# Output transposes of an attention kernel replaced by ones between V's columns and a swap of rows by DMA

## The chip, the cores and the metric

The kernel runs on one core of a Trainium2 chip. The core has five engines, each with its own queue of instructions that it works off in order: TensorE (PE in the profile, with its weight loads as PEld), VectorE (DVE), ScalarE (ACT), GpSimd (POOL) and SyncE (SP), which here only issues DMAs. They wait for each other through semaphores. The metric is the device time of one execution in microseconds; lower is better.

## What is computed

Cross-attention over 8 batches, 112 query rows, 375 key rows, width 256, 16 heads of 16 channels, all in 32-bit floats:

```python
Q = (x @ Wq.T + bq)      # per batch [112, 256], 16 heads of 16
K = (ctx @ Wk.T + bk)    # per batch [375, 256]
V = (ctx @ Wv.T + bv)    # per batch [375, 256]
scores = einsum('bhqd,bhkd->bhqk', Q, K) / sqrt(16)
attn = softmax(scores, axis=-1)
context = einsum('bhqk,bhkd->bhqd', attn, V)   # heads side by side: [112, 256]
z = context @ W_o.T + b_o + x
out = (z - mean(z)) / sqrt(var(z) + 1e-5) * gamma + beta   # over the 256 columns
```

## The kernel before

The work goes batch by batch (index `i`, 0 to 7), and a batch is cut into 12 units (`u`): 4 groups of 4 heads, each over 3 chunks of 125 key rows. In each unit TensorE computes one tile of scores with the keys on the partitions (L975, into `st_bank`), from which ScalarE makes the exponentials (L633, into `p_tile`, the tile that the profile calls `pw`). Beside that TensorE computes, some 17 heads ahead, the scores with the queries on the partitions (L942, into three `mx_bank`s), of which VectorE takes the maximum of each row (L748). The maxima of a batch are transposed (L957, "MT"), split in two parts and sent by DMA into a row of `q_stack` (L358), so that the scores of L975 come out already shifted by the maximum.

The projections of later batches lie between these: V of batch `i + 2` in units 2 to 4, K of batch `i + 3` in units 8 and 10 (L881). ScalarE takes each half of a K and rounds it (L545, L549), GpSimd subtracts (L430), and SyncE stacks the parts by DMA (L326) at the start of the next batch.

The product with V (L993) has 4 heads side by side in the array: head `j` of a group uses the array's columns from `32*j` on, with 16 columns of V and one column of ones (VW = 17), so that partition `32*j + 16` of `pv_bank` is the softmax denominator. In the batches 0 to 5 the products of two groups stand together in units 7 and, for the batch before, 1 (48 instructions); in batches 6 and 7 one group at a time (24 instructions).

What comes behind, for the batch whose products ended in unit 1 of the next batch: ScalarE copies `pv_bank` to `o_raw` (L604); TensorE transposes its four groups (L1004, "OT", in unit 6); VectorE takes the reciprocal of the 16 denominators of a row and multiplies (L770, L772, `normalise`); TensorE transposes the two halves back (L1012, mostly in front of MT, otherwise "ONT"); ScalarE copies them with V's bias to `o_normT` (L623); TensorE projects (L1025, "OUT", three batches later in unit 0; in the end sooner); VectorE adds the residual and takes mean and variance (L781 to L785); GpSimd does the rest of the layer norm (L450 to L467) and SyncE stores (L336).

The last batch but one ends inside batch 7: its last product with V is in unit 2, OUT(6) in unit 11. Batch 7's own output goes another way (L1037 to L1057), in quarters and halves. The order on every engine is written out by hand: loops over `i` and `u`, with tables that say which step stands in which unit (`U_OUT`, `U_OT`, `U_MT`). Two PSUM banks are handed from job to job in the order of `M0_JOBS` and `M1_JOBS`; a job waits until the one before it in its bank was read.

## Time and profile before

| | |
|---|---|
| median of 3 runs (141.05 to 143.31) | 141.18 us |
| the profiled execution | 142.0 us |
| its span, first to last instruction | 140.1 us |
| PE busy | 129.5 us (92%), 1477 instructions |
| DVE busy | 96.6 us (69%) |
| ACT busy | 90.1 us (64%) |
| POOL busy | 81.9 us (58%) |
| chain that ended last | PE 73%, SPq 9%, DVE 7%, DMA 5% |
| granted TensorE clock, mean | 0.993 |

Engines are named as above; SPq is SyncE's issuing of DMAs. A row of the timeline has its start and its length in microseconds from the span's start; instructions of one kind that follow each other are one row, with their count. On TensorE the lengths overlap, since a matmul's end is modelled, so the distance from one start to the next tells what a step costs. A 32-bit matmul is two instructions there (so L993 has 24 for the 12 matmuls of a group).

### The profile page before, as it was taken

Reading aid. Unit: us, or ns where it says so; the run is one execution under the profiler, and the core shown is the slowest. Engines: PE = TensorE matmul, PEld = TensorE weight load, DVE = VectorE, ACT = ScalarE, POOL = GpSimd, SP = SyncE. Lnnn points to the kernel's source line nnn. Section 1 sums busy time; section 2 is a strip of 40 time slices with the busy share of each in tenths; the row PEclk is TensorE's granted clock in tenths of the full one; section 3 lists DMA queues with packets and bytes.
Section 4 is the critical chain, followed back from the end, with each engine's and each line's share of the span. In section 5 each row is a group of like instructions: output and inputs, shape, how many; then the busy total and the mean of one; then the engine's idle time right before and its main releaser. Section 6 shows DMA issues by size and latency. Waiting matters only on the chain.

```text
span 140.1 us, 3936 instructions
## 1 busy us (share of the span) xinstructions
PE 129.5 (92%) x1477; PEld 113.6 (81%) x1477; DVE 96.6 (69%) x225; ACT 90.1 (64%) x187; POOL 81.9 (58%) x105
## 2 busy tenths in 40 slices
PE   4999997699999999998999999999999999999960
PEld 4799965589788979797989998999899888878720
...
GB/s 146 317 347 255 231 296 129 297 238 187 54 185 285 272 126 70 218 135 98 68 120 215 5 72 188 256 120 72 90 276 0 25 19 5 8 36 33 37 0 66
DMA packets 16099, 19.59 MB, mean 140 GB/s; under 512 B 2624, under 2 KB 15488, under 8 KB 16080
## 3 DMA queue, kind: packets, MB, share of 16 engines
...
q10 hardware_dynamic: 480, 0.28, 0.7%
q8 instruction: 12, 0.20, 0.7%
...
## 4 chain that ended last, share of the span: by engine, by line
PE 73%; SPq 9%; DVE 7%; DMA 5%; issue 3%; ACTq 1%; ACT 1%; POOLq 0%; DVEq 0%
PE m_bank L881 16%; PE pv_bank L993 14%; PE st_bank L975 14%; PE mx_bank L942 13%; PE m_bank L1025 4%; SPq L326 4%; SPq L266 4%; DMA q_stack<-shift_half 3%; PE m_bank L1004 2%; PE mx_bank L975 2%; DMA q_stack<-shift 2%; DVE k_stack L725 2%; DVE mx L748 2%; PE m_bank L902 1%; PE m_bank L1012 1%
## 5 line engine op out<-in xcount | busy, mean ns | idle before, releaser
L748 DVE TENSOR_REDUCE mx<-mx_bank 112x1 f32<-112x375 f32 x128 | 63.7, 541 | 22.3 <-PE mx_bank L942 21.9
L633 ACT ACTIVATE pw<-st_bank 125x448 f32<-125x448 f32 x86 | 45.1, 546 | 18.1 <-PE st_bank L975 17.8
L942 PE MATMUL mx_bank<-k_stack,q_stack 128*112 128x376 f32 x128 | 43.3, 352 | 0.2
L975 PE MATMUL st_bank<-q_stack,k_stack 128*125 128x224 f32 x172 | 34.9, 284 | 2.3 <-DMA q_stack<-shift_half 1.8
L975 PEld LDWEIGHTS st_bank<-q_stack,k_stack 128*125 128x125 f32 x172 | 28.5, 186 | 6.1 <-issue 3.6
L942 PEld LDWEIGHTS mx_bank<-k_stack,q_stack 128*112 128x112 f32 x128 | 22.0, 176 | 3.4 <-DVE mx L748 1.7
L430 POOL TENSOR_TENSOR k_hl<-k_full,k_hl 128x376 fp32r<-128x376 f32 x10 | 10.0, 1001 | 20.2 <-ACT k_hl L549 20.2
L993 PE MATMUL pv_bank<-pw,v_sb 125*17 125x112 f32 x744 | 21.5, 260 | 0.0
L993 PEld LDWEIGHTS pv_bank<-pw,v_sb 125*17 125x17 f32 x744 | 16.7, 97 | 3.1 <-issue 1.9
L881 PE MATMUL m_bank<-w_hl,c_hl 128*125 128x256 f32 x126 | 18.2, 282 | 0.0
L404 POOL TENSOR_TENSOR c_hl<-c_raw,c_hl 128x752 fp32r<-128x752 f32 x6 | 11.1, 1854 | 10.5 <-ACT c_hl L520 10.5
L881 PEld LDWEIGHTS m_bank<-w_hl,c_hl 128*125 128x125 f32 x126 | 17.3, 186 | 0.0
L881 PE MATMUL m_bank<-c_hl,w_hl 128*128 128x376 f32 x84 | 16.6, 335 | 0.3 <-DVE shift L755 0.3
L881 PEld LDWEIGHTS m_bank<-c_hl,w_hl 128*128 128x128 f32 x84 | 14.5, 188 | 0.5 <-DVE shift L755 0.5
L450 POOL TENSOR_SCALAR var_eps<-mv 112x1 f32<-112x1 f32 x7 | 1.6, 232 | 13.1 <-DVE mv L785 13.1
L461 POOL TENSOR_SCALAR yo<-z,mv,rstd 112x256 f32<-112x256 f32 x7 | 8.7, 1236 | 0.8
L559 ACT COPY v_sb<-m_bank 125x512 f32<-125x512 f32 (+1 forms) x14 | 6.8, 482 | 2.4 <-PE m_bank L881 1.9
L545 ACT ACTIVATE k_full<-m_bank,bqk 128x376 f32<-128x376 f32 x10 | 5.8, 576 | 3.8 <-PE m_bank L881 3.8
L1025 PE MATMUL m_bank<-wo,o_normT 128*112 128x256 f32 x28 | 7.4, 385 | 0.0
L604 ACT COPY o_raw<-pv_bank 128x448 f32<-128x448 f32 x7 | 3.7, 534 | 5.3 <-PE pv_bank L993 5.3
L781 DVE TENSOR_TENSOR z<-m_bank,x_space 112x256 f32<-112x256 f32 x7 | 2.9, 415 | 5.8 <-PE m_bank L1025 5.8
L633 ACT ACTIVATE pw<-mx_bank 125x448 f32<-125x448 f32 x10 | 5.3, 567 | 1.4 <-PE mx_bank L975 1.4
...
## 6 DMA issues: line engine op xcount, KB each, us to landing
...
```

What stands on the lines that cost most here:

```text
L404: nc.gpsimd.tensor_tensor(c_hl[b % 2][:, 1, :, :], c_raw[b % 2][:, :, :], c_hl[b % 2][:, 0, :, :].bitcast(F32), op=ALU.subtract).then_inc( ...
L430: nc.gpsimd.tensor_tensor(k_hl[b % 2][:, 1, t, :], k_full[:, t, :], k_hl[b % 2][:, 0, t, :].bitcast(F32), op=ALU.subtract).then_inc(k_lo, 1)
L461: nc.gpsimd.tensor_scalar(yo[b % 2][:, :], z[b % 2][:, :], mv[b % 2][:, 0:1], rstd[:, 0:1], op0=ALU.subtract, op1=ALU.mult).then_inc(y_rea ...
L545: nc.scalar.activation(k_full[:, t, :], src[:, 0:KVP], ACT.Identity, bias=bqk[:, 2 + t:3 + t]).then_inc(k_taken, 1)
L559: nc.scalar.copy(v_sb[b % VR][0:KC, c0:c0 + chunks, :, 0:DK], src[0:KC, 0:chunks * D].rearrange("p (c h d) -> p c h d", c=chunks, h=H)).th ...
L633: nc.scalar.activation(p_tile[0:KC, n % PR, :, :], st_of(n)[0:KC, 0:4 * Q].rearrange("p (j q) -> p j q", j=4), ACT.Exp, scale=float(DK) ** ...
L748: nc.vector.tensor_reduce(mx[b % 2][:, h % 2, q_pair(h // 2):q_pair(h // 2) + 1], mx_bank[n % MR][0:Q, 0:KV], axis=AX_X, op=ALU.max, negat ...
L881: last = nc.tensor.matmul(dst, lhs(a, e), rhs(c, e), start=(k + e == 0), stop=(k == len(PRODUCTS) - 1 and e == EC - 1))
L942: nc.tensor.matmul(mx_bank[n % MR][0:Q, 0:KVP], q_stack[k][:, side, q_pair(h // 2), b - Q_STACKS[k][0], :], k_stack[b % 3][:, h // 2, :], ...
L975: last = nc.tensor.matmul(st_of(n)[0:KC, k * 2 * Q:(k + 1) * 2 * Q], k_stack[i % 3][:, 2 * g + k, c * KC:(c + 1) * KC], q_stack[qk][:, :, ...
L993: last = nc.tensor.matmul(pv_of(b, g)[32 * j:32 * j + VW, g * Q:(g + 1) * Q], v_sb[b % VR][0:KC, c, 4 * g + j, :], p_tile[0:KC, (UNITS * b ...
L1025: last = nc.tensor.matmul(dst[0:Q, D:2 * D], o_normT[b % 2][:, k, :], wo[:, k, :], start=(k == 0), stop=(k == EC - 1))
```

## The change

V's tile gets 32 columns a head instead of 17: each of the 16 columns of V is followed by a column of ones (`VW = 2 * DK`). In `pv_bank` each even partition then holds a channel and the odd one behind it the denominator of the same head. The transposes OT and ONT and `normalise` go for batches 0 to 6. In their place, for batch `b`:

- ScalarE copies the whole bank to `o_raw` (`take_raw`, unit 1 of the next batch), then groups 0 and 2 to `o_normT` and groups 1 and 3 to `den` (`take_o`, unit 2). For batch 6 VectorE does all three (`take_o_last`, unit 2 of batch 7).
- SyncE sends two DMAs (`swap_rows`): the odd rows of groups 0 and 2 (denominators) into the even rows of `den`, and the even rows of groups 1 and 3 (channels) into the odd rows of `o_normT`. Then `o_normT` has 128 channels on its partitions, in an order for which the rows of W_o and the bias of V are permuted on the host, and `den` their denominators.
- VectorE takes the reciprocal of `den`, 128x224 (`invert`, unit 8; for batch 6 in unit 4 of batch 7).
- GpSimd multiplies and adds V's bias (`scale_output`), between its two subtractions for K.
- TensorE projects in unit 1, two batches later, in front of the products with V (for batch 4 in unit 8 of batch 6, for batch 5 in unit 5 of batch 7, for batch 6 in unit 11 of batch 7 as before). MT moves to unit 7, in front of the products with V (unit 4 in batch 6).

Ones are written once: VectorE's memset of the first V tile in two pieces, ScalarE's copy of the ones to the second, GpSimd's memset of the third. The memsets of `pv_bank` and `mx_bank` go, since all 128 partitions are now written. In batch 7, `normalise_last` has one reciprocal and one product for each group.

```diff
-VW = DK + 1
+VW = 2 * DK
...
-U_OUT, U_OT, U_Q, U_CONTEXT = 0, 6, 11, 5
+U_OUT, U_LN, U_Q, U_CONTEXT, U_NORM = 1, 1, 11, 5, 8
 U_K = ((9, 11), (8, 10))
 U_V = (2, 3, 4)
 HALF = UNITS // 2
-NORM_WITH = {3: 0, 4: 1, 5: 2, 6: 3, 7: 5}
-U_MT = (8, 7, 6, 6, 6, 6, 5)
+U_MT = (8, 7, 7, 7, 7, 7, 4)
+OUT_AT = {i: U_OUT for i in range(2, B - 2)} | {B - 2: 8, B - 1: 5}
+NORM_AT = {i: U_LN for i in range(2, B - 2)} | {B - 2: 8, B - 1: 5}
...
-    if _i >= 3:
-        M1_JOBS.append(("OUT", _i - 3))
+    if _i >= 2:
+        M0_JOBS.append(("OUT", _i - 2))
     M0_JOBS.append(("V", _i + V_AHEAD, 0))
     M1_JOBS.append(("V", _i + V_AHEAD, 1))
-    M0_JOBS.append(("MT", _i + 1))
-    M1_JOBS.append(("OT", _i - 1))
+    M1_JOBS.append(("MT", _i + 1))
...
-        v_sb = [sb(f"v_sb{i}", [PART, NC, H, VW]) for i in range(VR)]
+        v_sb = [sb(f"v_sb{i}", [PART, NC, H, DK, 2]) for i in range(VR)]
...
+            def swap_rows(b):
+
+                sp.wait_ge(o_raw_ready, b + 1)
+                raw = o_raw[b % 2][:, :].rearrange("p (e s q) -> p e s q", e=EC, s=2)
+                sp.dma_start(den[0:PART - 1:2, :, :], raw[1:PART:2, :, 0, :]).then_inc(swap_in[b % 2], 16)
+                sp.dma_start(o_normT[b % 2][1:PART:2, :, :], raw[0:PART - 1:2, :, 1, :]).then_inc(swap_in[b % 2], 16)
+
             for i in range(B):
                 if 1 <= i < B - V_AHEAD:
                     for t in range(2):
                         stack_k(i + V_AHEAD, t)
+                if i >= 1:
+                    swap_rows(i - 1)
...
+            nc.gpsimd.memset(v_sb[2][:, :, :, :, :], 1.0).then_inc(v_ones[2], 1)
...
+            def scale_output(b):
+
+                pool.wait_ge(rden_ready, b + 1)
+                nc.gpsimd.tensor_tensor(o_normT[b % 2][:, :, :], o_normT[b % 2][:, :, :], den[:, :, :],
+                                        op=ALU.mult).then_inc(o_scaled, 1)
+                pool.wait_ge(o_scaled, b + 1)
+                pool.wait_ge(bv_in, 16)
+                for e in range(EC):
+                    last = nc.gpsimd.tensor_scalar(o_normT[b % 2][:, e, :], o_normT[b % 2][:, e, :], bv[:, e:e + 1], None,
+                                                   op0=ALU.add)
+                last.then_inc(o_normT_ready, 1)
...
+                if 2 <= i < 2 + B // ROWS:
+                    bias_into_x(i - 2)
                 if i + AHEAD + 1 < B:
                     context_lo(i + AHEAD + 1)
                 if i == 0:
                     stack_q(pool, 2, 1)
                 if i + AHEAD < B:
-                    for t in range(2):
-                        subtract_k(i + AHEAD, t)
-                if 2 <= i < 2 + B // ROWS:
-                    bias_into_x(i - 2)
+                    subtract_k(i + AHEAD, 0)
+                if i >= 1:
+                    scale_output(i - 1)
+                if i + AHEAD < B:
+                    subtract_k(i + AHEAD, 1)
                 if i == 2:
                     clear_q()
             for b in range(B - V_AHEAD - 3, B - 1):
                 inverse_deviation(b)
                 scale_rows(b)
+                if b + 2 < B - 1:
+                    scale_output(b + 2)
...
-            def take_o(b):
+            def take_raw(b):
 
                 act.wait_ge(pv_done, NG * (b + 1))
                 if b >= 2:
-                    m, n = m_job("OT", b - 2)
-                    act.wait_ge(m_full[m], n + 1)
-                nc.scalar.copy(o_raw[b % 2][:, :], pv_bank[:, 0:NG * Q]).then_inc(o_raw_ready, 1)
+                    act.wait_ge(swap_in[b % 2], 32 * (b // 2))
+                nc.scalar.copy(o_raw[b % 2][:, :], pv_bank[:, 0:NG * Q])
+
+            def take_o(b):
+
+                src = pv_bank[:, 0:NG * Q].rearrange("p (e s q) -> p e s q", e=EC, s=2)
+                if b >= 2:
+                    wait_full(act, "OUT", b - 2)
+                nc.scalar.copy(o_normT[b % 2][:, :, :], src[:, :, 0, :])
+                if b >= 1:
+                    act.wait_ge(o_scaled, b)
+                nc.scalar.copy(den[:, :, :], src[:, :, 1, :]).then_inc(o_raw_ready, 1)
 
             def take_first_half():
...
-                    if u == (1 if i < B - 1 else 2) and i >= 1:
+                    if u == 1 and 1 <= i < B - 1:
+                        take_raw(i - 1)
+                    if u == 2 and 1 <= i < B - 1:
                         take_o(i - 1)
...
-            def normalise(b):
-
-                src = wait_full(dve, "OT", b)[0:Q, :].rearrange("p (h c) -> p h c", h=H)
-                nc.vector.reciprocal(rden[:, :, :], src[:, :, DK:VW]).then_inc(rden_ready, 1)
-                dve.wait_ge(rden_ready, b + 1)
-                nc.vector.tensor_tensor(o_norm[b % 2][:, :, :], src[:, :, 0:DK],
-                                        rden[:, :, :].to_broadcast([Q, H, DK]), op=ALU.mult
-                                        ).then_inc(o_norm_ready, 1)
+            def take_o_last():
+
+                b = B - 2
+                dve.wait_ge(pv_done, NG * (b + 1))
+                dve.wait_ge(swap_in[b % 2], 32 * (b // 2))
+                nc.vector.tensor_copy(o_raw[b % 2][:, :], pv_bank[:, 0:NG * Q])
+                src = pv_bank[:, 0:NG * Q].rearrange("p (e s q) -> p e s q", e=EC, s=2)
+                wait_full(dve, "OUT", b - 2)
+                nc.vector.tensor_copy(o_normT[b % 2][:, :, :], src[:, :, 0, :])
+                dve.wait_ge(o_scaled, b)
+                nc.vector.tensor_copy(den[:, :, :], src[:, :, 1, :]).then_inc(o_raw_ready, 1)
+
+            def invert(b):
+                dve.wait_ge(swap_in[b % 2], 32 * (b // 2 + 1))
+                nc.vector.reciprocal(den[:, :, :], den[:, :, :]).then_inc(rden_ready, 1)
...
+                    if u == U_NORM and 1 <= i < B - 1:
+                        invert(i - 1)
+                    if i == B - 1 and u == 2:
+                        take_o_last()
+                    if i == B - 1 and u == 4:
+                        invert(B - 2)
+                    if i >= 2 and u == NORM_AT[i]:
+                        layer_norm(i - 2)
+                    if i == B - 1 and u == 8:
                         layer_norm(B - 2)
...
-                                                v_sb[b % VR][0:KC, c, 4 * g + j, :],
+                                                v_sb[b % VR][0:KC, c, 4 * g + j, :, :].rearrange("k d s -> k (d s)"),
...
+                    if i + 1 < B and u == U_MT[i]:
+                        transpose_max(i + 1)
+                    if i >= 2 and u == OUT_AT[i]:
+                        out_project(i - 2)
...
-                    if u == U_OUT and i >= 3:
-                        out_project(i - 3 if i < B - 1 else B - 3)
-                    if u == 2 and i == 6:
-                        transpose_o_norm(4)
-                    if u == 3 and i == 6:
-                        transpose_o(5)
-                    if u == 5 and i == 6:
-                        out_project(4)
-                    if i + 1 < B and u == U_MT[i]:
-                        transpose_max(i + 1)
-                    if u == U_OT and 1 <= i <= 5:
-                        transpose_o(i - 1)
-                    if u == 4 and i == B - 1:
-                        transpose_o(B - 2)
-                    if u == 6 and i == B - 1:
-                        transpose_o_norm(B - 2)
...
-        "woT": w_o.T,
+        "woT": by_output(w_o.T),
```

TensorE's row in batch 4, units 6 and 7 (st_bank: scores; mx_bank: scores for the maximum; o_norm and o_raw: ONT and OT; mx: MT; pv_bank: products with V). Before:

```order
L942 MATMUL mx_bank<-k_stack,q_stack 112x376
L1012 MATMUL m_bank<-ident,o_norm 128x112 x2
L957 MATMUL m_bank<-ident,mx 16x112
L1004 MATMUL m_bank<-ident,o_raw 112x128 x4
L975 MATMUL st_bank<-q_stack,k_stack 125x224 x2
L942 MATMUL mx_bank<-k_stack,q_stack 112x376
L993 MATMUL pv_bank<-pw,v_sb 17x112 x24
```

and now:

```order
L999 MATMUL st_bank<-q_stack,k_stack 125x224 x2
L968 MATMUL mx_bank<-k_stack,q_stack 112x376
L981 MATMUL m_bank<-ident,mx 16x112
L1017 MATMUL pv_bank<-pw,v_sb 32x112 x24
L999 MATMUL st_bank<-q_stack,k_stack 125x224 x2
```

The six transposes are gone, MT stands in front of the products, and these have 32 rows out.

GpSimd's row from the end of batch 4 to batch 5 (k_hl: the two subtractions for K of batch 7; x_space: the output bias into the residual). Before:

```order
L430 TENSOR_TENSOR k_hl<-k_full,k_hl 128x376 x2
L437 TENSOR_TENSOR x_space<-x_space,bo_rows 112x256 x2
L450 TENSOR_SCALAR var_eps<-mv 112x1
```

and now:

```order
L445 TENSOR_TENSOR x_space<-x_space,bo_rows 112x256 x2
L438 TENSOR_TENSOR k_hl<-k_full,k_hl 128x376
L481 TENSOR_TENSOR o_normT<-o_normT,den 128x224
L486 TENSOR_SCALAR o_normT<-o_normT,bv 128x112 x2
L438 TENSOR_TENSOR k_hl<-k_full,k_hl 128x376
L458 TENSOR_SCALAR var_eps<-mv 112x1
```

The scaling of batch 3's output stands behind the first of K's subtractions, and TensorE's OUT(3) in unit 1 of batch 5 waits for it.

TensorE's row at the end, batch 7 from unit 8 on (o_normT: OUT(6)). Before:

```order
L975 MATMUL st_bank<-q_stack,k_stack 125x224 x2
L993 MATMUL pv_bank<-pw,v_sb 17x112 x12
L975 MATMUL st_bank<-q_stack,k_stack 125x224 x2
L975 MATMUL mx_bank<-q_stack,k_stack 125x224 x4
L1025 MATMUL m_bank<-wo,o_normT 112x256 x2
L993 MATMUL mx_bank<-pw,v_sb 17x112 x12
L1037 MATMUL m_bank<-ident,o_raw 112x128 x2
```

and now:

```order
L999 MATMUL st_bank<-q_stack,k_stack 125x224 x2
L1017 MATMUL pv_bank<-pw,v_sb 32x112 x12
L999 MATMUL st_bank<-q_stack,k_stack 125x224 x2
L999 MATMUL mx_bank<-q_stack,k_stack 125x224 x4
L1029 MATMUL m_bank<-wo,o_normT 112x256 x2
L1017 MATMUL mx_bank<-pw,v_sb 32x112 x12
L1041 MATMUL m_bank<-ident,o_raw 112x128 x2
```

OUT(6) keeps its place; what makes its input is now VectorE's three copies, two DMAs, a reciprocal and three GpSimd operations.

## Rows read from the trace of the kernel before

**Rows 1.** Windows: busy us (instructions) of each engine, then granted clock, DMA share.
```profile
100.00:125.00 25.00, 25.00 (x362) 21.54 (x364) 17.79 (x44) 17.62 (x40) 13.75 (x20) 1.00 0.18 59
125.00:140.00 15.00, 10.27 (x152) 7.00 (x140) 5.07 (x19) 6.76 (x17) 7.99 (x12) 0.94 0.11 32
```

**Rows 2.** Timeline of TensorE, batch 2, unit 6: start, length, then what.
```profile
63.93 0.38 PE L1012 MATMUL m_bank<-ident,o_norm 112*128 112x112 f32 x2 [0.37 <-issue]
64.15 0.26 PE L957 MATMUL m_bank<-ident,mx 112*16 112x112 f32 x1
```

**Rows 3.** Chain of work that ended last, batch 2: start, length, what.
```profile
64.41 0.44 PE m_bank L1004 x4
```

**Rows 4.** Groups by line and shape, weight loads: busy us, mean ns, idle before.
```profile
L993 PEld LDWEIGHTS pv_bank<-pw,v_sb 125*17 125x17 f32 x744 | 16.7, 97 | 3.1 <-issue 1.9 <-ACT pw L633 0.6
...
L975 PEld LDWEIGHTS st_bank<-q_stack,k_stack 128*125 128x125 f32 x172 | 28.5, 186 | 6.1 <-issue 3.6 <-ACT pw L633 1.1 <-DMA q_stack<-shift 0.8
```

**Rows 5.** Groups by line and shape, the other engines.
```profile
L437 POOL TENSOR_TENSOR x_space<-x_space,bo_rows 112x256 f32<-112x256 f32 x8 | 5.7, 734 | 0.0
...
L772 DVE TENSOR_TENSOR o_norm<-m_bank,rden 112x256 f32<-112x256 f32 x7 | 3.0, 424 | 0.2
...
L770 DVE RECIPROCAL rden<-m_bank 112x16 f32<-112x16 f32 x7 | 1.7, 243 | 1.4 <-PE m_bank L1004 1.4
...
L208 ACT COPY o_raw<-pv_bank 128x224 f32<-128x224 f32 x1 | 0.4, 381 | 0.0
...
L208 DVE COPY o_raw<-mx_bank 128x112 f32<-128x112 f32 x1 | 0.3, 254 | 0.0
...
L833 DVE RECIPROCAL rden<-m_bank 112x4 f32<-112x4 f32 x1 | 0.2, 183 | 0.1
```

**Rows 6.** Timelines: GpSimd's first subtraction and TensorE's products in unit 1.
```profile
54.57 1.02 POOL L430 TENSOR_TENSOR k_hl<-k_full,k_hl 128x376 fp32r<-128x376 f32 x1 [3.26 <-ACT k_hl L549]
57.45 1.34 PE L993 MATMUL pv_bank<-pw,v_sb 125*17 125x112 f32 x48
...
69.35 1.00 POOL L430 TENSOR_TENSOR k_hl<-k_full,k_hl 128x376 fp32r<-128x376 f32 x1 [3.19 <-ACT k_hl L549]
72.89 1.34 PE L993 MATMUL pv_bank<-pw,v_sb 125*17 125x112 f32 x48
...
98.65 1.00 POOL L430 TENSOR_TENSOR k_hl<-k_full,k_hl 128x376 fp32r<-128x376 f32 x1 [5.61 <-ACT k_hl L549]
101.67 1.34 PE L993 MATMUL pv_bank<-pw,v_sb 125*17 125x112 f32 x48
```

**Rows 7.** Timelines of ScalarE and TensorE, batch 6, units 1 to 4.
```profile
115.78 0.53 ACT L604 COPY o_raw<-pv_bank 128x448 f32<-128x448 f32 x1 [0.93 <-PE pv_bank L993]
116.32 0.55 ACT L633 ACTIVATE pw<-st_bank 125x448 f32<-125x448 f32 x1
...
117.60 0.77 PE L993 MATMUL pv_bank<-pw,v_sb 125*17 125x112 f32 x24
```

**Rows 8.** Timelines of all engines, batches 6 and 7, to the end.
```profile
120.26 1.14 SPq L358 DMA_DIRECT2D q_stack<-shift  x2
...
121.63 0.23 POOL L450 TENSOR_SCALAR var_eps<-mv 112x1 f32<-112x1 f32 x1 [1.58 <-DVE mv L785]
...
124.55 0.77 PE L993 MATMUL pv_bank<-pw,v_sb 125*17 125x112 f32 x24
...
125.46 0.23 POOL L450 TENSOR_SCALAR var_eps<-mv 112x1 f32<-112x1 f32 x1
...
130.03 1.03 PE L1025 MATMUL m_bank<-wo,o_normT 128*112 128x256 f32 x4
130.99 0.77 PE L993 MATMUL mx_bank<-pw,v_sb 125*17 125x112 f32 x24
...
137.26 0.48 DVE L860 SCALAR_TENSOR_TENSOR yo<-yo,rstd,be_rows 112x256 f32<-112x256 f32 x1 [0.40 <-POOL rstd L453]
```

**Rows 9.** DMAs by line: KB each, median us from issue to landing.
```profile
q_stack<-q_first SPq DMA_DIRECT2D x3, 56.0 KB, 2.3
```

More of the change, by code:

```diff
@@ L83 @@
         M0_JOBS.append(("Q", 3, _i - 1))
-M0_JOBS += [("OT", 5), ("MT", 7), ("OT", 6), ("OT_LAST", 0), ("OT_LAST", 2)]
-M1_JOBS += [("OUT", 3), ("ONT", 4), ("OUT", 4), ("OUT", 5), ("ONT", 6), ("OUT", 6), ("OUT", B - 1)]
+M0_JOBS += [("OUT", 4), ("OT_LAST", 0), ("OT_LAST", 2)]
+M1_JOBS += [("MT", 7), ("OUT", 5), ("OUT", 6), ("OUT", B - 1)]
 S0_JOBS += [("ONT_HALF", 0), ("ONT_HALF", 1)]
@@ L140, in build @@
         rden = sb("rden", [Q, H, 1])
-        o_norm = [sb(f"o_norm{i}", [Q, H, DK]) for i in range(2)]
+        o_norm = sb("o_norm", [Q, EC, 4, DK, 2])
+        den = sb("den", [PART, EC, Q])
         o_normT = [sb(f"o_normT{i}", [PART, EC, Q]) for i in range(2)]
@@ L174, in build @@
         ident_clear, ident_ready = sem("ident_clear"), sem("ident_ready")
-        pv_clear = sem("pv_clear")
         k_ones = [sem(f"k_ones{i}") for i in range(3)]
         q_clear = [sem(f"q_clear{k}") for k in range(NQ)]
-        v_ones = sem("v_ones")
+        warm_ready, v_ones = sem("warm_ready"), [sem(f"v_ones{i}") for i in range(VR)]
         m_full = [sem(f"m_full{i}") for i in range(len(JOBS))]
@@ L186, in build @@
         o_raw_ready, rden_ready = sem("o_raw_ready"), sem("rden_ready")
-        o_norm_ready, o_normT_ready = sem("o_norm_ready"), sem("o_normT_ready")
+        o_scaled, o_normT_ready = sem("o_scaled"), sem("o_normT_ready")
+        swap_in = [sem(f"swap_in{i}") for i in range(2)]
         xb_ready = sem("xb_ready")
@@ L615, in take_half_t @@
                                      bias=bv[:, k:k + 1]).then_inc(half_normT, 1)
-            def take_o_norm_t(b, *job):
-                src = wait_full(act, *job)
-                if job[0] == "MT":
-                    act.wait_ge(shift_ready, job[1] + 2)
-                act.wait_ge(bv_in, 16)
-                for k in range(EC):
-                    last = nc.scalar.activation(o_normT[b % 2][:, k, :], src[:, k * Q:(k + 1) * Q], ACT.Identity,
-                                                bias=bv[:, k:k + 1])
-                last.then_inc(o_normT_ready, 1)
             for i in range(B):
@@ L738, in _ @@
             context_lo(1)
-            for i in range(1, VR):
-                nc.vector.memset(v_sb[i][:, :, :, DK:VW], 1.0).then_inc(v_ones, 1)
             for t in range(2):
@@ L830, in normalise_last @@
                 g0, n = LAST[k].start, LAST[k].stop - LAST[k].start
[L831 to L833 removed]
+                src = (wait_full(dve, "OT_LAST", k)[0:Q, 0:n * PART]
+                       .rearrange("p (g j d s) -> p g j d s", g=n, j=4, s=2))
+                scale = rden[:, 4 * g0:4 * (g0 + n), :].rearrange("p (g j) x -> p g j x", g=n)
+                to = o_norm[:, g0 // 2, :, :, g0 % 2:g0 % 2 + n].rearrange("p j d s -> p s j d")
+                for g in range(n):
+                    last = nc.vector.reciprocal(scale[:, g], src[:, g, :, 0, 1:2])
+                last.then_inc(rden_ready, 1)
                 dve.wait_ge(rden_ready, B + k)
[L835 to L837 removed]
+                for g in range(n):
+                    last = nc.vector.tensor_tensor(to[:, g], src[:, g, :, :, 0], scale[:, g].to_broadcast([Q, 4, DK]),
+                                                   op=ALU.mult)
+                last.then_inc(last_norm, 1)
             dve.wait_ge(pv_done, NG * (B - 1) + LAST[1].stop)
[L840 removed]
+            dve.wait_ge(swap_in[(B - 1) % 2], 32 * ((B - 1) // 2))
             take_last(nc.vector.tensor_copy, 1)
@@ L998, in values @@
                     last.then_inc(pv_done, 1)
-            def transpose_o(b):
-                dst, full = claim("OT", b)
-                pe.wait_ge(o_raw_ready, b + 1)
-                for g in range(NG):
-                    last = nc.tensor.transpose(dst[0:Q, g * PART:(g + 1) * PART],
-                                               o_raw[b % 2][:, g * Q:(g + 1) * Q], ident[:, :])
-                last.then_inc(full, 1)
-            def norm_columns(dst, b):
-                pe.wait_ge(o_norm_ready, b + 1)
-                flat = o_norm[b % 2][:, :, :].rearrange("q h d -> q (h d)")
-                for k in range(EC):
-                    last = nc.tensor.transpose(dst[:, k * Q:(k + 1) * Q], flat[:, k * PART:(k + 1) * PART],
-                                               ident[0:Q, 0:Q])
-                return last
-            def transpose_o_norm(b):
-                dst, full = claim("ONT", b)
-                norm_columns(dst, b).then_inc(full, 1)
             def out_project(b):
@@ L1144, in by_stack, with by_output @@
     return a.reshape(2, 4, 2, DK, *rest).transpose(0, 2, 3, 1, *range(4, 4 + len(rest))).reshape(D, *rest)
+def by_output(a):
+    rest = a.shape[1:]
+    return a.reshape(EC, 2, 4, DK, *rest).transpose(0, 2, 3, 1, *range(4, 4 + len(rest))).reshape(D, *rest)
 def kernel(x, ctx_1024, L0_xattn_W_qkv, L0_xattn_b_qkv, L0_xattn_W_o, L0_xattn_b_o, L0_xattn_ln_gamma,
```

59 lines of the change are left out of this document (13 added, 46 removed).

## The prediction, written before the changed kernel was run

> **What bounds the kernel now.** I read the page first, then the chain of waits, then TensorE's timeline batch by batch, then each queue that the change touches. In the windows TensorE is busy through all of 100 to 125 us at the granted clock 1.00, its level of 2.4 GHz, while VectorE, ScalarE and GpSimd stand at 18, 18 and 14 of 25 us [rows 1]. The page's slices show the same from the second quarter of the span on. So an instruction taken from TensorE in this stretch is worth its whole length, and a wait put into TensorE's row costs its whole length. After 125 us TensorE is busy 10.3 of 15 us [rows 1]: there the end is a chain through several engines, and lengths of steps count, whoever does them.
>
> **What goes from TensorE.** ONT's two transposes are 0.22 us from start to start [rows 2], OT's four are 0.44 us on the chain [rows 3]: 0.66 us a batch. In front of ONT in batch 2 TensorE also stood 0.37 us for the head maxima [rows 2]; MT one unit later no longer meets that. Up to batch 6 OT of batches 0 to 4 and ONT of 0 to 3 go: 5 x 0.44 + 4 x 0.22 + 0.37 = 3.45 us.
>
> **Wider weights.** The stationary tile of a product with V has 32 columns instead of 17. A load of 17 columns takes 97 ns, one of 125 takes 186 [rows 4]: 0.82 ns a column, so 12 ns more for each of 768 loads (744 in this row, 24 in another bank). But 24 loads of 97 ns are 2.3 us, and the 24 products with their loads take 0.77 us [rows 8], so loads run under matmuls of the other three heads. At the least this costs nothing; if each load showed its 12 ns it would be 9.4 us. I take the first load of each of some 20 bursts, 0.25 us, since the row with the same array layout hides its loads. The Trainium skill says (TensorE: Matmul & The Clock Gate, LDWEIGHTS (loading the stationary operand)) that a load takes columns / 1.2 ns: 14 ns for 17, 27 for 32, an estimate; all 768 exposed would then come to 9.6 us. The trace's rows have nearly the same slope on a far larger constant, and do not show the loads exposed [rows 4, 8].
>
> **A new wait in unit 1.** OUT(i-2) needs `scale_output(i-2)`, which GpSimd does after the first subtraction for K, and this waits for K's projection in unit 8. `scale_output`: one product over 224 columns, 0.70 us (256 columns take 0.734 [rows 5]); two additions over 112 columns, for which no row is near; with one input and half the columns they lie between 0.37 and 0.73, and I take 0.48; 0.2 us for three handoffs. Sum 1.86 us, bounds 1.6 to 2.4. In batch 5 TensorE would start OUT(3) where the products now start, less the OUT that leaves unit 0 (0.96 us from start to start [rows 8]): 101.67 - 0.96 = 100.7. GpSimd is ready at 98.65 + 1.00 + 1.86 = 101.5 [rows 6]. TensorE waits 0.8 us, and the products, which stand behind OUT, with it. Batch 4 has the same spacing. In batches 2 and 3 a projection of Q lengthens the unit before: 54.57 + 1.02 + 1.86 = 57.45, just when the products start now (batch 2 has no OUT in unit 0 to lose), so nothing; 69.35 + 1.00 + 1.86 = 72.2 against 72.89 - 0.96 = 71.9, 0.3 us [rows 6]. Together 1.9 us. Each GpSimd price off by 0.3 us moves this by up to 1 us. VectorE's reciprocal in unit 8 ends before GpSimd asks for it.
>
> **Batch 6.** The products of its first group need the bank empty. ScalarE's first copy starts at 115.78 and takes 0.53, an exponential 0.55 [rows 7], then two copies of 0.38 each (128x224 took 0.381 [rows 5]): 117.6 us, when the products start now [rows 7]. So the 0.66 us of transposes in front of them gain nothing. Behind them go ONT(5), 0.22, and OUT(5), which moves past the last products of batch 6: 1.18 us. In batches 1 to 5 ScalarE's 0.76 us more lie in its idle time before unit 3.
>
> **At the end of batch 6's products (E).** They end at 124.55 + 0.77 = 125.3 us now [rows 8]; then at 125.3 - 3.45 - 1.18 + 0.25 + 1.9 = 122.8.
>
> **From E to OUT(6).** VectorE's copies: 112 columns take 0.254, 256 take 0.424 [rows 5], so 0.65 for 448 and 0.39 for each 224: 1.43 us. SyncE issues two DMAs, 0.57 each [rows 8], and the second lands 2.3 us after its issue began, as the DMA of rows of the same length does [rows 9]: 2.87. The reciprocal: 4 columns 183 ns, 16 columns 243 [rows 5], 5 ns a column, so 1.28 us for 224; at the least it runs like a copy, 0.39. `scale_output` 1.86, handoffs 0.2. Sum 7.64 us: OUT(6) starts at 130.5, against 130.03 now [rows 8]. TensorE's own work between is 4.7 - 0.66 + 0.96 = 5.0 us, so it stands idle for 2.6 us, and the last products with V are behind OUT(6) in its row. OUT(6) is 0.45 us later than now.
>
> **GpSimd's backlog.** `scale_output(6)` stands in front of two layer norms of 125.46 - 121.63 = 3.83 us each [rows 8], which start only then: 7.7 us, and then comes the last deviation, 0.6 us, for which VectorE's last operation waits. It starts 8.2 us after OUT(6) starts, against 137.26 - 130.03 = 7.23 now [rows 8]: 1.0 us.
>
> **Edits without cost.** The memsets and the copy of ones run before the data has arrived or beside it. GpSimd's third memset delays K(2) on TensorE, which at that place waits for the first shift anyway; without that cover it would cost its own length. SyncE's two issues stand behind K's stacking and, in batch 6, ahead of the shift for batch 7, 1.14 us for such a pair [rows 8]; the shift then still has seven units until it is asked for. `bias_into_x` moves into GpSimd's idle time.
>
> **Sum.** 0.45 + 1.0 = 1.45 us later. The profiled execution of 142.0 us (span 140.1) would become 143.4; it stands 0.8 over the median of the runs, 141.18, so the forecast is 142.6 us, 1% slower: what is taken from TensorE comes back as waits for GpSimd and at the end.
>
> **Rivals.**
> 1. *The waits are short.* Reciprocal like a copy (-0.9), additions at 0.37 (-0.2 from E to OUT(6), -0.2 in each of three batches): -1.7, 140.9 us, and 139.8 if the additions cost still less. For: the rows of the reciprocal read single PSUM elements far apart, and the slope may be that of the reading. Against: GpSimd's chain in batches 4 and 5 is late with any price of the additions. Chance 0.20.
> 2. *All of it is saved*: no wait in unit 1, and the way from E to OUT(6) is covered. 7 x 0.66 + 0.37 = 5.0 us: 136.2. This needs the 7.64 us to fit into 5.0, by two missing terms at once. Chance 0.04.
> 3. *The wider weights show.* If the four loads of a round cannot overlap, each round grows by one load's 12 ns or all four: 2.4 to 9.4 us, 145 to 152 us. It decides from the point where four loads no longer fit under one round of matmuls. Chance 0.08.
> 4. *The clock falls in the wait before OUT(6).* TensorE stands still for 2.6 us there, and in the last stretch the granted clock is already 0.94 on average [rows 1]; at 1.2 GHz OUT(6) alone takes 0.96 us more, and with the products and transposes behind it some 3 us: 146. Against: TensorE's present waits leave the clock full up to 125 us [rows 1]. The Trainium skill (TensorE: Matmul & The Clock Gate, Part 1: The HAM clock gate) has the clock halved after a stretch without matmuls. This trace shows a fall only in its last stretch [rows 1]. Chance 0.08.
>
> **How the numbers follow.** The forecast's case has the remaining 0.60, with 141.0 to 144.6 as its own range (the reciprocal and the additions up or down by half of their bounds). This kernel's measurement can tell about 2%, 138.4 to 144.0 us, from no change. Faster: rival 2 and a little, 0.05. Slower: rivals 3 and 4 and the upper fifth of the forecast's case, 0.28. The rest, 0.67, is no change. The range goes from the lower end of rival 1 to the lower ends of 3 and 4: 139.8 to 145.6.
>
> **What would show it.** Right: TensorE's OUT rows in batches 4 and 5 preceded by 0.5 to 1.2 us of idle time that GpSimd's `o_normT` ends; idle time of 2 to 3 us before OUT(6); VectorE's reciprocal of `den` near 1.3 us; GpSimd's last power 8 us behind OUT(6). Wrong: rounds of the products with V above their present pace (0.77 us for 24), reciprocals of 0.4 us, OUT in unit 1 without idle time, or a granted clock below 1.00 before 125 us.

## The result: 5.3% slower

The changed kernel takes 149.54 us (median of 4 runs, 147.66 to 149.67), the kernel before 141.28 us on the same chip: ratio 1.0531, 95% interval 1.0466 to 1.0596. The ratio is an estimate of its own and not the quotient of the two medians (1.058). Ratios leave out runs in a slower state, more than 1.5% above the fastest of their kernel. The profiled execution took 149.67 us, its span is 147.9 us (140.1 before). The windows of [rows 1], of the changed kernel (TensorE, weight loads, VectorE, ScalarE, GpSimd, clock):

```profile
100.00:125.00 25.00, 22.84 (x321) 18.48 (x319) 17.34 (x35) 16.54 (x37) 13.41 (x20) 1.00 0.21 70
125.00:148.00 23.00, 14.36 (x172) 9.63 (x164) 9.02 (x28) 7.30 (x17) 14.45 (x22) 0.85 0.09 26
```

TensorE, busy all of the first window before, stands 2.2 of 25 us; the second has grown from 15 to 23 us, and its clock is 0.85 on average. What TensorE waited for from 41 to 131 us, in waits of over 0.15 us (total us, times, longest):

```profile
PE st_bank L999 <- ACT pw L659: 1.3, 2, 0.7
PE mx_bank L968 <- DVE mx L767: 1.0, 1, 1.0
PE st_bank L999 <- DMA q_stack<-shift: 0.4, 1, 0.4
PE m_bank L1029 <- DVE q_hl L733: 0.3, 2, 0.2
PE m_bank L981 <- DVE mx L767: 0.3, 1, 0.3
```

None of these is GpSimd's `o_normT`. The first two are the places to look at. Unit 1 of batch 5, TensorE, ScalarE and GpSimd (start, length, what, idle time before it):

```profile
100.87 0.51 PE L968 MATMUL mx_bank<-k_stack,q_stack 128*112 128x376 f32 x2
102.02 0.48 PE L999 MATMUL st_bank<-q_stack,k_stack 128*125 128x224 f32 x2 [0.65 <-ACT pw L659]
102.34 0.34 PE L968 MATMUL mx_bank<-k_stack,q_stack 128*112 128x376 f32 x1
102.58 1.09 PE L1029 MATMUL m_bank<-wo,o_normT 128*112 128x256 f32 x4
103.60 1.36 PE L1017 MATMUL pv_bank<-pw,v_sb 125*32 125x112 f32 x48
...
100.42 0.57 ACT L570 ACTIVATE k_full<-m_bank,bqk 128x376 f32<-128x376 f32 x1
101.02 0.51 ACT L574 CAST k_hl<-k_full 128x376 fp32r<-128x376 f32 x1
101.43 1.65 ACT L659 ACTIVATE pw<-st_bank 125x448 f32<-125x448 f32 x3
...
101.36 1.12 POOL L486 TENSOR_SCALAR o_normT<-o_normT,bv 128x112 f32<-128x112 f32 x2
```

The same place in the kernel before:

```profile
100.06 1.12 PE L1025 MATMUL m_bank<-wo,o_normT 128*112 128x256 f32 x4
100.83 0.53 PE L942 MATMUL mx_bank<-k_stack,q_stack 128*112 128x376 f32 x1
101.19 0.37 PE L975 MATMUL st_bank<-q_stack,k_stack 128*125 128x224 f32 x2
101.41 0.34 PE L942 MATMUL mx_bank<-k_stack,q_stack 128*112 128x376 f32 x1
```

ScalarE works off two conversions of K (1.1 us) before the exponentials of units 11 and 0 free the next `st_bank`. Before, OUT lay between the scores of units 0 and 1 and covered just this time; now it stands behind them, and TensorE waits 0.65 us bare. GpSimd's `o_normT` was ready at 102.48, only 0.1 us too late, because the other wait had come first. Without that wait TensorE would have come to OUT some 0.65 us sooner, at about 101.9 (an estimate from these rows), and would have stood nearly as long for GpSimd: two waits lie beside each other here.

A shorter wait of the same kind, below the list's 0.15 us, stands in unit 7 of the batches 2 to 5. In batch 5, first before, with MT and six transposes ahead of the unit's scores, then in the changed kernel:

```profile
107.62 0.36 PE L1012 MATMUL m_bank<-ident,o_norm 112*128 112x112 f32 x2
...
108.26 0.46 PE L975 MATMUL st_bank<-q_stack,k_stack 128*125 128x224 f32 x2
```

```profile
109.37 0.34 PE L968 MATMUL mx_bank<-k_stack,q_stack 128*112 128x376 f32 x1
109.78 0.48 PE L999 MATMUL st_bank<-q_stack,k_stack 128*125 128x224 f32 x2
110.10 0.33 PE L968 MATMUL mx_bank<-k_stack,q_stack 128*112 128x376 f32 x1
```

From 109.37 to 109.78 are 0.41 us where the pace is 0.17, and the unit's two score instructions take 0.32 where two take 0.21: 0.34 us lost, though TensorE stood only 0.07 us for an exponential (the trace names ScalarE). Before, the transposes lay over this time.

And the end of batch 5 on VectorE:

```profile
112.43 0.55 DVE L767 TENSOR_REDUCE mx<-mx_bank 112x1 f32<-112x375 f32 x1 [0.95 <-PE mx_bank L968]
112.89 1.54 DVE L800 RECIPROCAL den<-den 128x224 f32<-128x224 f32 x1
114.35 1.84 DVE L767 TENSOR_REDUCE mx<-mx_bank 112x1 f32<-112x375 f32 x4
```

The reciprocal stands in front of four head maxima; no projections are left in this batch with which TensorE could pass the time, all three `mx_bank`s fill, and it stands 1.0 us. VectorE had idled 0.95 us just before.

The changed operations by line and shape (busy us, mean ns), to be read beside [rows 4, 5]:

```profile
L1017 PEld LDWEIGHTS pv_bank<-pw,v_sb 125*32 125x32 f32 x744 | 17.6, 111 | 4.6 <-issue 2.6 <-ACT pw L659 1.4
L800 DVE RECIPROCAL den<-den 128x224 f32<-128x224 f32 x7 | 10.8, 1547 | 6.5 <-DMA o_normT<-o_raw 6.5
L486 POOL TENSOR_SCALAR o_normT<-o_normT,bv 128x112 f32<-128x112 f32 x14 | 7.8, 568 | 0.7
L481 POOL TENSOR_TENSOR o_normT<-o_normT,den 128x224 f32<-128x224 f32 x7 | 4.7, 666 | 13.4 <-DVE den L800 13.4
```

The chain of waits from batch 6's last products to OUT(6):

```profile
125.97 0.76 PE pv_bank L1017 x24
...
126.75 0.62 DVE o_raw L791
127.38 0.30 DVE o_normT L794
127.68 0.31 DVE den L796
...
128.00 0.67 SPq L363
...
128.71 3.04 DMA o_normT<-o_raw
...
135.38 2.02 PE m_bank L1029 x4
```

Between 131.8 and 135.4 come the reciprocal (1.55 us) and GpSimd's three operations (1.87). TensorE ran out of work at 131.5. The clock (the number ahead of the DMA share) in that wait, and from OUT(6) on:

```profile
131.50:133.50 2.00, 0.01 (x1) 0.00 (x0) 1.72 (x2) 1.27 (x4) 0.08 (x1) 1.00 0.19 57
135.50:140.50 5.00, 5.00 (x55) 3.09 (x55) 1.92 (x8) 0.00 (x0) 4.46 (x7) 0.50 0.07 23
```

The clock fell from 1.00 to 0.50 (2.4 to 1.2 GHz) at about 134.7 us, while TensorE stood still, and came back at about 141.1, when it had been at work since 135.4. OUT(6) takes 2.02 us where it took 1.03 [rows 8].

**Where the 7.8 us of span came from.** Batch 6's products end at 126.7 (125.3 before): +1.4. From there to OUT(6) 8.65 us instead of 4.7: +3.95. From OUT(6) to the end 12.5 instead of 10.1: +2.4. The first part by kinds of TensorE's work, from batch 1 to the end of batch 6's products. Each instruction counts from the end of the one before it to its own end, both as the profile models them, and idle time stands apart; predicted for idle time are 1.9 in unit 1 and 0.66 in batch 6, less the 0.37 of [rows 2]:

| us | before | after | predicted change | change |
|---|---|---|---|---|
| transposes OT, ONT | 4.15 | 0 | -3.96 | -4.15 |
| OUT (6 before, 5 after) | 5.37 | 5.11 | -0.96 | -0.26 |
| MT | 0.67 | 0.90 | 0 | +0.23 |
| products with V | 16.85 | 17.01 | +0.25 | +0.16 |
| scores | 35.86 | 38.59 | 0 | +2.73 |
| projections | 20.50 | 20.24 | 0 | -0.26 |
| idle | 0.98 | 3.88 | +2.19 | +2.90 |

The scores' 2.73 us belong for the most part to the waits: the first score behind idle time ends 0.37 us after its start, where one that follows another ends 0.11 us behind it (0.43 and 0.17 for the scores of the maxima), so a wait costs 0.26 us more than its idle time. Twelve scores stand behind idle time in the changed kernel, three before. Nine of the twelve waited for ScalarE's exponentials: 1.7 us idle and nine times 0.26, some 4.1 us together, as much as the transposes gave. The kernel before had one or two such waits, with no more than 0.01 us idle in each.

Distances from one start to the next mislead behind OUT: in front of scores its four instructions take 0.77 us to the next start in the rows above (0.67 in other batches), but the score behind them takes 0.36 to the next start instead of 0.17. From end to end OUT costs 0.86 to 0.96 us in the kernel before, whatever follows it.

### The profile page after: what moved, and what is told of

Its sections match the earlier page's. It is cut to its first block, busy times and chain, and to the rows that moved or that the text cites. A ratio compares the mean times of both kernels' runs of the same rounds, so it can differ in the third digit from the quotient of the medians.

```text
span 147.9 us, 3872 instructions
## 1 busy us (share of the span) xinstructions
PE 130.5 (88%) x1435; PEld 110.8 (75%) x1435; DVE 103.6 (70%) x220; ACT 90.0 (61%) x185; POOL 95.1 (64%) x127
## 4 chain that ended last, share of the span: by engine, by line
PE 54%; DVE 12%; ACT 9%; issue 9%; POOL 8%; DMA 4%; ACTq 1%; SPq 1%; POOLq 0%; DVEq 0%
PE pv_bank L1017 13%; PE m_bank L907 13%; PE mx_bank L968 9%; PE st_bank L999 9%; ACT pw L659 5%; PE m_bank L1029 5%; ACT k_full L570 3%; DVE mx L767 3%; POOL q_stack L264 2%; POOL q_stack L406 2%; DMA o_normT<-o_raw 2%; DMA q_stack<-shift 2%; DVE k_stack L746 2%; POOL c_hl L412 1%; DVE den L800 1%
## 5 line engine op out<-in xcount | busy, mean ns | idle before, releaser
L968 PE MATMUL mx_bank<-k_stack,q_stack 128*112 128x376 f32 x128 | 42.0, 348 | 2.7 <-issue 1.5
L1017 PE MATMUL pv_bank<-pw,v_sb 125*32 125x112 f32 x744 | 22.3, 266 | 0.0
L1017 PEld LDWEIGHTS pv_bank<-pw,v_sb 125*32 125x32 f32 x744 | 17.6, 111 | 4.6 <-issue 2.6
L800 DVE RECIPROCAL den<-den 128x224 f32<-128x224 f32 x7 | 10.8, 1547 | 6.5 <-DMA o_normT<-o_raw 6.5
L481 POOL TENSOR_TENSOR o_normT<-o_normT,den 128x224 f32<-128x224 f32 x7 | 4.7, 666 | 13.4 <-DVE den L800 13.4
L1029 PE MATMUL m_bank<-wo,o_normT 128*112 128x256 f32 x28 | 8.5, 430 | 4.2 <-issue 3.9
L630 ACT COPY o_raw<-pv_bank 128x448 f32<-128x448 f32 x6 | 3.2, 534 | 10.0 <-PE pv_bank L1017 10.0
L1029 PEld LDWEIGHTS m_bank<-wo,o_normT 128*112 128x112 f32 x28 | 4.8, 193 | 5.9 <-issue 4.2
L486 POOL TENSOR_SCALAR o_normT<-o_normT,bv 128x112 f32<-128x112 f32 x14 | 7.8, 568 | 0.7
```

The lines of the kernel that those rows point to most:

```text
L486: last = nc.gpsimd.tensor_scalar(o_normT[b % 2][:, e, :], o_normT[b % 2][:, e, :], bv[:, e:e + 1], None, op0=ALU.add)
L800: nc.vector.reciprocal(den[:, :, :], den[:, :, :]).then_inc(rden_ready, 1)
L968: nc.tensor.matmul(mx_bank[n % MR][0:Q, 0:KVP], q_stack[k][:, side, q_pair(h // 2), b - Q_STACKS[k][0], :], k_stack[b % 3][:, h // 2, :], ...
L1017: last = nc.tensor.matmul(pv_of(b, g)[32 * j:32 * j + VW, g * Q:(g + 1) * Q], v_sb[b % VR][0:KC, c, 4 * g + j, :, :].rearrange("k d s -> k ...
L1029: last = nc.tensor.matmul(dst[0:Q, D:2 * D], o_normT[b % 2][:, k, :], wo[:, k, :], start=(k == 0), stop=(k == EC - 1))
```

## Experiments

Ratios are to the kernel before on the same chip, with 95% intervals.

**1. scale_first**: is it GpSimd that is waited for?

```diff
-                if i + AHEAD < B:
-                    subtract_k(i + AHEAD, 0)
                 if i >= 1:
                     scale_output(i - 1)
                 if i + AHEAD < B:
+                    subtract_k(i + AHEAD, 0)
                     subtract_k(i + AHEAD, 1)
```

> GpSimd scales the batch's output before both subtractions of K's low parts instead of between them, so o_normT is ready about 1.0 us (one 999 ns subtraction) earlier. Theory of the prediction: the output projection in unit 1 waits for the scaling, so the changed kernel should gain up to 1.9 us, 149.5 to about 147.6. Theory from its trace (the 0.65 us of TensorE in unit 1 of batches 4 and 5 end with ScalarE's exponentials, not with GpSimd): no change, 149.5 within 0.5 us, and the 0.65 us stay.

Measured 149.04 us, ratio 1.0511 (1.0476 to 1.0546): no gain that can be told from none. The waits of ScalarE's making are unchanged:

```profile
PE st_bank L998 <- ACT pw L658: 1.3, 2, 0.7
```

Units 1 of batches 4 and 5 are 0.14 us shorter, which is all that stood behind GpSimd alone there. Whether TensorE would wait for GpSimd if it did not wait for ScalarE, this run can't tell; experiments 2 and 3 bear on it.

**2. out_before**: the edit of experiment 1, and the projection back behind unit 0's scores.

```diff
-U_OUT, U_LN, U_Q, U_CONTEXT, U_NORM = 1, 1, 11, 5, 8
+U_OUT, U_LN, U_Q, U_CONTEXT, U_NORM = 0, 1, 11, 5, 8
```

> The same earlier scaling, and in batches 2 to 5 the output projection behind unit 0's first scores, where the kernel before had it in batches 3 to 5, not in unit 1. Theory 'lost cover': the projection's 0.96 us on TensorE lay over ScalarE's two K conversions (0.57 + 0.51 us) that stand ahead of the exponentials of unit 0; put back, the 0.65 us of batches 4 and 5 go, and the 0.17 us of batches 2 and 3: 1.6 us less, about 147.9, and unit 1 to unit 2 takes 2.0 us again (3.1 now). Theory 'wait for GpSimd': with the scaling 1.0 us earlier and the projection 1.0 to 1.5 us earlier the wait is as long as before, 149.5, and shows in front of the projection. Third: batch 5's end is set by VectorE (its reciprocal), which gives back part: 148.5.

Measured 149.03 us, 1.0504 (1.0444 to 1.0564): missed. The waits for ScalarE in unit 1 are gone and batches 4 and 5 are 0.3 and 0.5 us shorter, but two others took their place:

```profile
PE m_bank L1028 <- DVE q_hl L732: 2.0, 2, 1.0
...
PE m_bank L1028 <- issue: 0.6, 2, 0.3
```

In batches 2 and 3 OUT's PSUM bank held a projection of Q until VectorE had read it (batches 0.55 us longer each); in 4 and 5 OUT now waits 0.3 us for its input.

**3. out_cover**: the edit of experiment 1, and the projection back in batches 4 and 5 alone.

```diff
-OUT_AT = {i: U_OUT for i in range(2, B - 2)} | {B - 2: 8, B - 1: 5}
+OUT_AT = {2: U_OUT, 3: U_OUT, 4: 0, 5: 0} | {B - 2: 8, B - 1: 5}
```

> The changed kernel with the scaling ahead of both subtractions on GpSimd, and with the output projection behind unit 0's first scores in batches 4 and 5 only (2 and 3 keep unit 1, since there it waited 1.0 us for VectorE's low parts of Q when it was moved). Theory 'cover and GpSimd together': batches 4 and 5 take 0.5 us less each, 149.5 to 148.5, with 0.3 us of wait for GpSimd left in each. If neither wait matters to the end: 149.5.

Measured 148.37 us, 1.0467 (1.0381 to 1.0554): 1.2 us under the changed kernel's median, about as expected, but the intervals overlap. Batches 4 and 5 take 14.88 and 14.02 us from start to start, 15.05 and 14.56 in the changed kernel: the expected 0.5 us came in batch 5 only. OUT still waits 0.3 us for its input in each, with GpSimd's scaling a whole subtraction earlier.

**4. before_out_late**: the same move, alone, in the kernel before.

```diff
-                    if u == U_OUT and i >= 3:
+                    if u == U_OUT and i >= B - 2:
...
+                    if u == U_OUT + 1 and 3 <= i < B - 2:
+                        out_project(i - 3)
                     if i == B - 1 and u in (5, 8, 11):
```

> The kernel before, with one thing changed: in batches 3 to 5 the output projection stands in unit 1 in front of the products with V instead of behind unit 0's scores. No swap, no reciprocal of 224 columns, transposes as before, and the projection's input is ready long ahead. Theory 'lost cover': TensorE stands 0.65 us in unit 1 of batches 4 and 5 for ScalarE's exponentials (as in the changed kernel), and the products with V start 0.25 us later behind the projection than behind scores: 2 x 0.65 + 3 x 0.25 = 2.0 us more, 141.9 to about 143.9. Theory 'only its input was late': no change, 141.9.

Measured 143.82 us, 1.0144 (1.0077 to 1.0210): 2.0 us slower by the ratio, as 'lost cover' had it. Its batch 5 on TensorE, with no swap and no GpSimd in the way:

```profile
101.76 0.48 PE L975 MATMUL st_bank<-q_stack,k_stack 128*125 128x224 f32 x2 [0.66 <-ACT pw L633]
...
102.25 1.02 PE L1025 MATMUL m_bank<-wo,o_normT 128*112 128x256 f32 x4
103.20 1.34 PE L993 MATMUL pv_bank<-pw,v_sb 125*17 125x112 f32 x48
```

The 0.66 us are there. From start to start the batches 3, 4 and 5 are 0.30, 0.82 and 0.80 us longer than before, 1.9 together. The reason is not the expectation's 0.25 us for the place in front of the products: OUT ends 0.86 us behind the score ahead of it in all three, no later than before. It is the waits for ScalarE (0.04, 0.64 and 0.66 us idle) and the 0.26 us that each costs on top.

**5. no_reciprocal**

```diff
-                nc.vector.reciprocal(den[:, :, :], den[:, :, :]).then_inc(rden_ready, 1)
+                nc.vector.reciprocal(den[:, :, 0:1], den[:, :, 0:1]).then_inc(rden_ready, 1)
```

> The reciprocal of the denominators covers 1 column (of 128x224, 1547 ns, seven times), so the outputs of batches 0 to 6 are multiplied by denominators that were mostly not inverted; everything else stands. Theory 'the reciprocal is on the path twice': the 1.0 us that TensorE waits for a head maximum at the end of batch 5 goes, and the wait ahead of the last batch's output projection (3.9 us) shrinks by 1.4 us: 2.4 us less, 147.1, with the clock still falling; if the shorter wait also keeps the granted clock at 1.00, up to 2.4 us more, 144.7. Theory 'hidden, the swap alone counts': under 0.5 us less, 149.0 to 149.5.

Measured 145.98 us, 1.0284 (1.0241 to 1.0326): 3.6 us less, between the two cases of its first theory. The wait for a head maximum is gone; the wait ahead of OUT(6) is 2.6 us, and the clock still falls, but comes back sooner:

```profile
133.00:136.00 3.00, 3.00 (x30) 1.68 (x28) 1.31 (x4) 0.00 (x0) 2.72 (x4) 0.52 0.00 0
136.00:140.00 4.00, 3.39 (x36) 1.79 (x34) 1.78 (x9) 0.96 (x3) 3.54 (x6) 1.00 0.09 29
```

**6. invert_early**

```diff
-U_OUT, U_LN, U_Q, U_CONTEXT, U_NORM = 1, 1, 11, 5, 8
+U_OUT, U_LN, U_Q, U_CONTEXT, U_NORM = 1, 1, 11, 5, 7
```

> VectorE's reciprocal moves from unit 8 to behind the shift in unit 7, where VectorE idles for 0.95 us in batch 5 while TensorE does products with V. Theory 'the reciprocal stands in front of a head maximum at the end of batch 5': of TensorE's 1.0 us there 0.6 to 1.0 us goes, 149.5 to about 148.7. Rival: in batches 2 to 4 it now delays the maximum that ends the next wait and the gain is paid back there, 149.5.

Measured 147.80 us, 1.0345 (1.0245 to 1.0445): 1.7 us less by the medians. The single runs spread too far to weigh that: 146.6, 146.7, 148.9 and 149.3, against 147.7, 149.5, 149.6 and 149.7 of the changed kernel, 1.1 us less at the lowest and 0.4 at the highest. Batch 5 takes 13.53 us instead of 14.56, 1.0 us less, as expected. The rest of the 3.1 us that its profile's span gains lies elsewhere, in what the edit does not touch: batch 1 began 0.6 us sooner, batch 6's second swap DMA landed 2.72 us after its issue (3.04 in the changed kernel), and from OUT(6) to the end are 11.3 us instead of 12.5, since the clock fell only behind OUT(6)'s start and OUT(6) took 1.09 us.

**7. busy_wait**: the clock alone.

```diff
+                        idle_bank, _ = claim("OT_LAST", 0)
+                        for _ in range(8):
+                            nc.tensor.matmul(idle_bank[0:Q, 0:D], ident[:, 0:Q], wo[:, 0, :], start=True, stop=True)
                         out_project(B - 2)
```

> Eight fp32 products of 112x256 into a free PSUM bank (two instructions of 0.216 us each, 3.45 us) run on TensorE in the 3.9 us wait ahead of OUT(6); nothing waits for them. Theory 'the clock': it stays at 1.00, OUT(6) starts where it did (135.4) and takes 1.0 us instead of 2.02, the products behind it 0.77 instead of 1.35; the end comes earlier by 1.4 us (148.1) if GpSimd's two layer norms (8.2 us behind OUT(6)) then end last, by 2.4 us (147.1) if TensorE does. Theory 'the work behind OUT(6) is bound by GpSimd anyway': no change, 149.5.

Measured 147.81 us, 1.0413 (1.0374 to 1.0453): 1.7 us less, for work that nobody uses. Windows of the wait and of what follows:

```profile
131.50:135.30 3.80, 3.80 (x22) 3.15 (x21) 2.44 (x4) 1.68 (x5) 2.01 (x5) 1.00 0.10 30
135.30:140.50 5.20, 5.09 (x64) 3.11 (x64) 2.53 (x12) 0.96 (x3) 4.64 (x8) 1.00 0.07 22
```

The clock stands at 1.00 in the wait and behind it. Its timeline there:

```profile
135.34 1.03 PE L1029 MATMUL m_bank<-wo,o_normT 128*112 128x256 f32 x4
...
143.35 0.48 DVE L886 SCALAR_TENSOR_TENSOR yo<-yo,rstd,be_rows 112x256 f32<-112x256 f32 x1 [1.16 <-POOL rstd L461]
```

OUT(6) starts where it did and takes 1.03 us. Now GpSimd ends last: VectorE's last operation waits for its `rstd` and starts 8.0 us after OUT(6) (9.7 in the changed kernel, 7.23 before [rows 8]).

**8. last_by_transposes**: batch 6's output as in the kernel before, on the wider V.

```diff
+M0_JOBS += [("OUT", 4), ("OT", 6), ("OT_LAST", 0), ("OT_LAST", 2)]
+M1_JOBS += [("MT", 7), ("OUT", 5), ("ONT", 6), ("OUT", 6), ("OUT", B - 1)]
...
-                if i >= 1:
+                if 1 <= i < B - 1:
                     swap_rows(i - 1)
...
+                    if u == 4 and i == B - 1:
+                        transpose_o(B - 2)
+                    if u == 6 and i == B - 1:
+                        transpose_o_norm(B - 2)
```

> The changed kernel, but batch 6's output goes by transposes as in the kernel before (V keeps its 32 columns; four transposes, one reciprocal of 16 columns, multiplications, two transposes, ScalarE's copies with the bias), so there is no swap, no 224-column reciprocal and no scaling on GpSimd between the last products of batch 6 and OUT(6). Theory 'the tail': from those products to OUT(6) 4.8 us instead of 8.8, the granted clock stays at 1.00 and returns 2.4 us behind it: 6.0 us less on top of 0.5 us for the six transposes, 149.5 to 143.5. Theory 'the loss lies in the batches before': under 1.5 us less, 148.

Measured 143.68 us, 1.0129 (1.0056 to 1.0201): 5.9 us less. The scores ahead of OUT(6) run into it without a gap:

```profile
131.69 0.60 PE L1021 MATMUL mx_bank<-q_stack,k_stack 128*125 128x224 f32 x4
132.12 1.03 PE L1051 MATMUL m_bank<-wo,o_normT 128*112 128x256 f32 x4
```

**9. all_mended**: the edits of 1, 6 and 8 together, OUT behind unit 0's scores in batches 2 to 5, and the banks of OUT and MT exchanged.

```diff
     if _i >= 2:
-        M0_JOBS.append(("OUT", _i - 2))
+        M1_JOBS.append(("OUT", _i - 2))
...
-    M1_JOBS.append(("MT", _i + 1))
+    M0_JOBS.append(("MT", _i + 1))
...
+OUT_AT = {i: 0 for i in range(2, B - 2)} | {B - 2: 8, B - 1: 5}
```

> All four repairs in the changed kernel: batch 6's output by transposes, the scaling ahead of both subtractions, the projection behind unit 0's scores in batches 2 to 5 (it changes PSUM banks with the maxima's transpose, so that it waits for no low part of Q), the reciprocal in unit 7. From the runs: 143.7 with the last batch by transposes, less 1.0 (cover, as in out_cover), less 1.0 (TensorE's wait for the reciprocal in batch 5), less 0.9 for batches 2 and 3 (0.28 us of products behind the projection and 0.17 us of wait in each): 140.8, against 142.0 of the kernel before, ratio 0.992. Theory 'the repairs overlap': the waits hide behind each other and 1.5 us or less is gained, 142.2, ratio 1.00.

Measured 139.82 us, **1.4% faster than the kernel before** (0.9862, 0.9835 to 0.9889): a version that beats both. From the start of batch 1 to that of batch 6 it takes 69.6 us (71.1 in the kernel before), and its end is that of the kernel before (10.05 us from OUT(6) on, against 10.07). What TensorE waits for from 41 to 134 us, in waits of over 0.15 us:

```profile
PE m_bank L1002 <- DVE mx L781: 0.3, 1, 0.3
PE m_bank L1058 <- DVE o_raw L805: 0.2, 1, 0.2
PE mx_bank L989 <- DVE mx L781: 0.2, 1, 0.2
```

**10. all_mended2**: MT moved again.

```diff
+                    if i + 1 < B and u == U_MT[i] and i > 0:
+                        transpose_max(i + 1)
                     for h in heads[:1]:
                         scores_for_max(h)
```

> all_mended, with the maxima's transpose in front of unit 7's (batch 6: unit 4's) first scores for the next maxima, so that it no longer stands directly in front of the products with V. In the changed kernel that place took 0.19 us where it took 0.10 before: 6 x 0.09 = 0.5 us less than all_mended, 140.3. Rival: the transpose itself now waits for the last maximum, up to 0.5 us in each batch, 141 or more.

Measured 140.12 us, 0.9888 (0.9854 to 0.9922): no gain over all_mended, and not the rival's 141 either. To the next start MT takes 0.03 us instead of 0.19 in batches 2 to 5, but the score that now stands last in front of the products takes 0.33 where 0.17 is its pace, and TensorE waits 0.3 us once more for a maximum.

## Why the prediction was wrong, step by step

The forecast was 142.6 us, no change; 149.5 is outside its range. The direction of its sum (gains on TensorE given back as waits and at the end) held, its sizes did not: against +1.45 us it was +7.8. Of the 6.3 us between, 3.9 arose before the end of batch 6's products (E), 1.0 from there to OUT(6), 1.4 behind it.

- **Held: transposes and weights.** -4.15 us against -3.96, each instruction taken from end to end. The load of 32 columns takes 111 ns against 97 for 17 [rows 4], and all products with V together cost 0.16 us more against a forecast of 0.25; rival 3 falls. The Trainium skill's slope for weight loads (TensorE: Matmul & The Clock Gate, LDWEIGHTS (loading the stationary operand)), 1 ns for 1.2 columns, gives 12.5 ns for the 15 more columns, an estimate. The rows show 14, and hidden.
- **Failed: "an instruction taken from TensorE in this stretch is worth its whole length."** The forecast took no account of waits for ScalarE that OUT and the transposes lay over. With them gone or moved, TensorE stood nine times for an exponential, some 4.1 us in all, and what the transposes gave came back. In unit 1 of batches 4 and 5 this is shown by experiment 4, with no swap and no GpSimd in the way; in unit 7 it is read from the trace alone, and no run puts only the transposes back.
- **Failed: "TensorE waits 0.8 us" for `scale_output` in unit 1.** The size nearly held (0.65 us, in batches 4 and 5) and GpSimd's price did (1.87 us against 1.86), but that is luck: the wait that ended last was ScalarE's. GpSimd's lay beside it, and the forecast's own sign of being wrong came true: OUT in unit 1 has next to no idle time ahead of it. Experiment 1 moves GpSimd and not ScalarE and gains nothing that can be told; no run moves ScalarE's wait alone.
- **Failed: the gain from one OUT fewer**, 0.26 us instead of 0.96. The price was right (0.86 to 0.96), but the five OUTs left cost 0.86 to 1.12 each, since in unit 1 their input or their bank came late. MT's place in front of the products cost nothing by itself: whatever stands last in front of the products with V takes 0.09 us more to the next start, the scores before (0.26 against 0.17) as MT now (0.19 against 0.10).
- **Failed: "VectorE's reciprocal in unit 8 ends before GpSimd asks for it."** True for the projections in unit 1, and the wrong question: behind it on VectorE are the head maxima, for which TensorE waits 1.0 us in batch 5 (gone in experiment 5, 0.16 us in experiment 6).
- **Mis-sized: from E to OUT(6).** 8.65 us instead of 7.64: the two DMAs 3.76 instead of 2.87, the reciprocal 1.55 instead of 1.28; the copies took 1.23 against 1.43, and the scaling as forecast.
- **Rival 4 came true**, with 0.08: the clock fell in that wait, which was 3.9 us and not 2.6, from 1.00 to 0.50. The Trainium skill has the clock halved when TensorE goes idle (TensorE: Matmul & The Clock Gate, Part 1: The HAM clock gate); the trace agrees. The forecast priced it at some 3 us; experiment 7 gives 1.7, since GpSimd's backlog (8.2 us forecast, 8.0 measured there) ends nearly as late.

Experiment 8 weighs the parts: by the ratios, 4.0 of the 5.3 points go with the swap of one batch, the last that has one (5.9 of 8.3 us by the medians). Left open: why the second DMA of the last two swaps took 2.7 to 3.9 us to land in these runs, when the median of the seven is 1.9 to 2.1.
